# Gate probabilities of the top two logits: two sigmoids on ScalarE in place of a difference, an exponential with sum, and a reciprocal

## The chip, the cores and the metric

The kernel runs on one core of a Trainium2 chip. The metric is the device time of one execution in microseconds (us), as the median of several runs. The engines are TensorE (PE in the profile, with its weight loads as PEld), VectorE (DVE), ScalarE (ACT), GpSimd (POOL) and SyncE (SP), which here only issues DMAs.

## The reference

The input x is 8 tiles of 128 tokens by 512 features. A linear layer with a per-tile LoRA adapter comes first, then a feed-forward layer with a mixture of 8 LoRA experts, of which each token uses its two best. Cut to what matters:

```python
# cond: base layer plus the adapter of this tile
base_out = jnp.einsum('bsi,io->bso', x, W)
lora_out = jnp.einsum('bsr,bro->bso', jnp.einsum('bsi,bir->bsr', x, A), Bm)
c = base_out + lora_out
# ffn, E=8 experts, R=16, TOP_K=2, SCALING=1.0
result = jnp.einsum('bnd,od->bno', c, W_base) + b_base
logits = jnp.einsum('bnd,ed->bne', c, W_gate)
probs = jax.nn.softmax(logits, axis=-1)
top_p, top_i = jax.lax.top_k(probs, TOP_K)
top_p = top_p / jnp.sum(top_p, axis=-1, keepdims=True)
route_w = jnp.sum(jax.nn.one_hot(top_i, E) * top_p[..., None], axis=-2)
h = jnp.einsum('bnd,erd->bner', c, A_ffn)
delta = jnp.einsum('bner,eor->bno', h * route_w[..., None], B)
return x + result + delta * SCALING
```

Only the ratio of the two best probabilities survives the division by their sum. With the two largest logits v0 and v1, the two weights are 1/(1+exp(v1-v0)) and exp(v1-v0)/(1+exp(v1-v0)), which are sigmoid(v0-v1) and sigmoid(v1-v0).

## The kernel before, in words

All matmuls are made of three products of operands that are split in a high and a low part (x_hi and x_lo and so on): lines 811, 812 and 813 are the three products of the helper `product`. ScalarE writes the high parts, VectorE subtracts them from the raw values to get the low parts (the helper `lo`, line 597).

Up to about 28 us both layers are folded into one matrix. Then the 8 tiles (t = 0 to 7) are worked on in pairs (q = 0 to 3). The first two pairs (q = 0, 1 in the names `Left`, `Right`) are plain; pairs 2 and 3 use seven products in place of eight (`M1` to `M7`). For each pair TensorE forms the left bank of each tile (which holds the 8 logits, the 128 values h and part of the output), transposes the adapter activations (`T1`, line 923), and adds their contribution (`Lora_left`, line 937, which reports lg_done; `Lora_right`, line 944). From then on the logits of both tiles are complete and the gate can run. The gate gives hw, the 128 values h times the expert weights. TensorE transposes hw (`T2(t)`, line 954) into one single bank that all tiles share, ScalarE casts it to hw_hi (line 511), VectorE subtracts to get hw_lo (`split_hw`, line 597), and `Delta(t)` adds the experts' output.

The order of work on every engine is written out by hand, in five programs; engines wait for each other by semaphores. What matters here:

- `T2(t)` waits for hw_done(t+1), that is for the gate of its own tile, and for hw_lo_done(t), that is for the low split of the tile before it, since both use the one bank. It stands in TensorE's queue between other products; if it waits, everything behind it waits.
- VectorE's queue: gate(0), gate(1), split_x_inner(2), split_xa(2), split_hw(0), split_xa(3), split_hw(1), split_cs(SUM1), then gate(2), gate(3), sum_e(2) (line 686), split_cs(SUM7) (cs_lo, line 597), split_xa(4) (lines 721 and 723), split_hw(2), and so on; at the end split_xd(3), gate(6), gate(7), split_hw(6), sum_u1(3), split_hw(7).
- ScalarE's queue around gates 2 and 3: copy_left(0), copy_left(1), exp_top(2), copy_right(0), copy_right(1), copy_m5(2) (line 524), exp_top(3), copy_m4(2) (line 528, which waits for `M4(2)` on TensorE), split_hw(2) (line 511), split_cs(SUM7), split_cs(SUM6) (line 484). sum_e(2) waits for copy_m4(2); the VectorE split_cs(SUM7) waits for ScalarE's.
- TensorE's queue: ... Left(2), T2(0), Left(3), T2(1), Delta(0), T1(1), Delta(1), Lora_left(1), M5(2), M4(2), T2(2), M3(2), M2(2), T2(3), Right(2), ..., M7(3), M6(3, first chunk), Lora_right(3), T2(7), Delta(6), M6(3, second chunk), Lora_right(3), Delta(7).

The gate of one tile on VectorE (`gate`, lines 731 to 751) is nine instructions in the trace: the eight largest logits in order (line 736, MAX8), their first two minus the first (line 737, a TENSOR_SCALAR with a scalar from memory), the positions of the largest (line 739, which the trace shows as MATCH_VALUE_LOAD and FIND_INDEX8), the comparison of the expert numbers with the two positions (line 740), the reciprocal of the sum (line 743), the one-hot rows times the exponentials (line 744), the sum of both rows (line 746), and h times the weights times the reciprocal (line 749, a SCALAR_TENSOR_TENSOR with a scalar from memory). ScalarE's `exp_top` (line 504) takes the exponential of the two differences and adds them up; the trace shows an ACTIVATE and an ACTIVATION_READ_ACCUMULATOR. The helper `step` makes VectorE wait for its own instruction before it issues the next.

Of the kernel before, what the change touches and what calls it, by code (L numbers as in the profile page):

```python
# [5 lines left out]
F32 = mybir.dt.float32  # L6
F32R = mybir.dt.float32r
U32 = mybir.dt.uint32
ALU = mybir.AluOpType
ACT = mybir.ActivationFunctionType  # L10

P = 128
# [3 lines left out]
R = 16  # L16
NA = 16
E = 8
# [6 lines left out]
TOP = 2  # L25
# [17 lines left out]
def adaln_ffn_kernel(nc, x_t, itok, fold_in, lora, ffn_b, bias, out):  # L43
    ctx = ExitStack()
    with ctx:
        def sb(name, shape, dt=F32):
            return ctx.enter_context(nc.sbuf_tensor(name, shape, dt))

        def sem(name):
            return ctx.enter_context(nc.semaphore(name))  # L50
# [39 lines left out]
        top_val = sb("top_val", [P, 2, 8])  # L90
        top_idx = sb("top_idx", [P, 2, 8], U32)
        top_diff = sb("top_diff", [P, 2, TOP])
        top_exp = sb("top_exp", [P, 2, TOP])
        top_sum = sb("top_sum", [P, 2, 1])
        top_rcp = sb("top_rcp", [P, 2, 1])
        onehot = sb("onehot", [P, 2, TOP, E])
        weighted = sb("weighted", [P, 2, TOP, E])
        route = sb("route", [P, 2, E])
        hw = sb("hw", [P, 2, ER])
# [3 lines left out]
        table_warm = sb("table_warm", [P, 1])  # L103
# [5 lines left out]
        def part(flat, at, *shape):  # L109
# [62 lines left out]
            sem("left_done"), sem("xa_hi_done"), sem("xa_done"), sem("t1_done"), sem("xa_t_done"))  # L172
        lg_done, lz_done, gate_step, diff_done, exp_done, hw_done = (
            sem("lg_done"), sem("lz_done"), sem("gate_step"), sem("diff_done"), sem("exp_done"), sem("hw_done"))
        t2_done, hw_hi_done, hw_lo_done = sem("t2_done"), sem("hw_hi_done"), sem("hw_lo_done")
# [31 lines left out]
        def left(t):  # L207
            return left_bank[t % 4]
# [204 lines left out]
        def scalar_program(act):  # L413
            act.dma_start(w_raw[:, 0, FIRST:D + GH], fold_in[0, :, FIRST:D + GH]).then_inc(w_first_loaded, DMA)
            nc.scalar.activation(table_warm[:], nc.const_aps.tensor(0.0, [P, 1], F32), ACT.Exp)
            act.wait_ge(w_first_loaded, DMA)
# [84 lines left out]

            def exp_top(t):
                act.wait_ge(diff_done, t + 1)
                nc.scalar.activation(top_exp[:, t % 2], top_diff[:, t % 2], ACT.Exp,  # L504
                                     accum_out=top_sum[:, t % 2]).then_inc(exp_done, 1)

# [27 lines left out]
            copy_xa_t(0)  # L534
            split_x_inner(2)
            exp_top(0)
            exp_top(1)
            act.wait_ge(x4_lo_done, 1)
# [9 lines left out]
            copy_left(1)  # L548
            exp_top(2)
            copy_right(0)  # L550
            copy_right(1)
            copy_m5(2)
            exp_top(3)
            copy_m4(2)
# [10 lines left out]
            copy_xa_t(2)  # L565
            exp_top(4)
            copy_left(2)
            copy_right(2)
            copy_left(3)
            copy_right(3)  # L570
            exp_top(5)
            copy_m5(3)
# [6 lines left out]
            copy_xa_t(3)  # L579
            exp_top(6)  # L580
            copy_left(4)
            copy_right(4)
            exp_top(7)
            copy_right(5)
# [8 lines left out]
        def vector_program(dve):  # L593
# [113 lines left out]
            def step(instruction):  # L707
                instruction.then_inc(gate_step, 1)
                steps[0] += 1
                dve.wait_ge(gate_step, steps[0])  # L710
# [20 lines left out]
            def gate(t):  # L731
                n = t % 2
                logits = left(t)[:, gate_cols(t)]
                h = left(t)[:, h_cols(t)].rearrange("p (e r) -> p e r", e=E)
                dve.wait_ge(lg_done, t // 2 + 1)
                step(nc.vector.max(top_val[:, n], logits))
                nc.vector.tensor_scalar(top_diff[:, n], top_val[:, n, 0:TOP], top_val[:, n, 0:1], None,  # L737
                                        ALU.subtract).then_inc(diff_done, 1)
                step(nc.vector.max_index(top_idx[:, n], top_val[:, n], logits))
                step(nc.vector.tensor_tensor(onehot[:, n], expert_id[:].unsqueeze(1).broadcast_to([P, TOP, E]),  # L740
                                             top_idx[:, n, 0:TOP].unsqueeze(2).broadcast_to([P, TOP, E]), ALU.is_equal))
                dve.wait_ge(exp_done, t + 1)
                nc.vector.reciprocal(top_rcp[:, n], top_sum[:, n])
                step(nc.vector.tensor_tensor(weighted[:, n], onehot[:, n],
                                             top_exp[:, n].unsqueeze(2).broadcast_to([P, TOP, E]), ALU.mult))
                step(nc.vector.tensor_tensor(route[:, n], weighted[:, n, 0, :], weighted[:, n, 1, :], ALU.add))
                if t >= 2:
                    dve.wait_ge(t2_done, t - 1)
                nc.vector.scalar_tensor_tensor(out=hw[:, n].rearrange("p (e r) -> p e r", e=E), in0=h,  # L749
                                               scalar=top_rcp[:, n], in1=route[:, n].unsqueeze(2).broadcast_to([P, E, R]),  # L750
                                               op0=ALU.mult, op1=ALU.mult).then_inc(hw_done, 1)

# [374 lines left out]
```

## Time and profile before

| what | value |
|---|---|
| median of 3 runs | 66.19 us |
| the 3 runs | 66.19, 65.9, 66.25 us |
| the profiled execution | 65.62 us |
| its span, first to last instruction | 64.4 us |
| what lies around the span | 1.2 us |
| mean granted TensorE clock | 1.000 |
| TensorE busy | 59.6 us, 92% |
| VectorE busy | 49.2 us, 76% |
| ScalarE busy | 34.2 us, 53% |
| GpSimd busy | 23.7 us, 37% |

The times in the rows of the profile are from this one profiled execution and are counted from the start of its span. A matmul's row lasts from its start until its modelled end; the next one starts before that, since they are pipelined. So TensorE's progress is read from the starts of successive rows, or from the chain of waits, in which each piece is only what that matmul adds.

### The profile page before, as it was taken

To read this page: it belongs to the slowest core of one execution; us is meant where nothing else is said; L and a number is where in the kernel's file an instruction comes from. 1 tells how busy PE (TensorE), PEld (TensorE's weight loads), DVE (VectorE), ACT (ScalarE), POOL (GpSimd) and SP (SyncE) were. 2 spreads that over 40 slices of the span, in tenths; PEclk is the share of its full clock that TensorE was granted. 3 is DMA by queue.
4 is the path that set the end of the run, shared out by engine and by line. 5 is a ranking of instruction groups with operands and counts; after the bars stand their busy time and mean duration, and the time that the engine had idled before them with its cause. 6 is when DMAs were issued, how large, how long until landed. Compare 5 with 4: busy or idle time off the path is not lost.

```text
span 64.4 us, 1331 instructions
## 1 busy us (share of the span) xinstructions
PE 59.6 (92%) x406; PEld 58.0 (90%) x406; DVE 49.2 (76%) x154; ACT 34.2 (53%) x91; POOL 23.7 (37%) x46
## 2 busy tenths in 40 slices
PE   4979999999999999999999999979999999999900
PEld 4969999999999999999998999959999999998800
DVE  0948689955799989999889748969788668887510
ACT  1754689807399577074161756847094723355220
POOL 1000999798400799997039960000000000001300
DMA  0799999700998106233331323630008000023371
GB/s 0 210 362 300 371 377 404 276 0 20 320 294 320 42 12 188 60 73 63 66 81 37 72 62 74 222 132 0 0 0 300 29 6 0 0 89 116 121 279 52
DMA packets 5529, 8.75 MB, mean 136 GB/s; under 512 B 1009, under 2 KB 2065, under 8 KB 5522
## 3 DMA queue, kind: packets, MB, share of 16 engines
q1 hardware_dynamic: 4978, 7.88, 38.4%
q0 software_dynamic: 256, 0.52, 2.2%
q10 hardware_dynamic: 288, 0.27, 1.2%
q8 instruction: 3, 0.05, 0.3%
q14 instruction: 4, 0.03, 0.2%
HBM read 5.26 MB, written 2.10 MB: 114 GB/s over the span
## 4 chain that ended last, share of the span: by engine, by line
PE 81%; DVE 6%; DMA 5%; issue 2%; ACT 1%; DVEq 0%
PE bank L811 19%; PE bank L813 19%; PE bank L812 19%; PE bank L819 8%; PE bank L821 5%; DMA w_raw<-fold_in 5%; PE bank L985 3%; PE bank L937 2%; PE bank L954 2%; PE bank L944 1%; PE bank L989 1%; DVE cs_lo L597 1%; PE bank L923 1%; DVE top_diff L737 1%; DVE hw L749 1%
## 5 line engine op out<-in xcount | busy, mean ns | idle before, releaser
L811 PE MATMUL bank<-c_hi,x_hi 128*128 128x408 f32 (+1 forms) x40 | 13.6, 339 | 0.0
L812 PE MATMUL bank<-c_lo,x_hi 128*128 128x408 f32 (+1 forms) x40 | 13.4, 334 | 0.0
L813 PE MATMUL bank<-c_hi,x_lo 128*128 128x408 f32 (+1 forms) x40 | 13.4, 334 | 0.0
L398 POOL TENSOR_TENSOR x_raw<-x_raw 128x256 f32<-128x256 f32 x1 | 0.7, 739 | 21.3 <-DVE x_raw L703 21.3
L597 DVE TENSOR_TENSOR x_lo<-x_raw,x_hi 128x512 fp32r<-128x512 f32 (+1 forms) x10 | 7.8, 808 | 0.0
L811 PEld LDWEIGHTS bank<-c_hi,x_hi 128*128 128x128 f32 x40 | 7.5, 188 | 0.1
L812 PEld LDWEIGHTS bank<-c_lo,x_hi 128*128 128x128 f32 x40 | 7.5, 188 | 0.0
L813 PEld LDWEIGHTS bank<-c_hi,x_lo 128*128 128x128 f32 x40 | 7.5, 188 | 0.0
L331 POOL DMA_DIRECT2D lora_raw<-lora x8 | 4.4, 554 | 6.1 <-issue 5.9
L504 ACT ACTIVATE top_exp<-top_diff 128x2 f32<-128x2 f32 x8 | 1.6, 203 | 8.1 <-DVE top_diff L737 8.1
L811 PE MATMUL bank<-ffn_b_hi,hw_hi 128*128 128x256 f32 x16 | 4.8, 298 | 0.0
L813 PE MATMUL bank<-ffn_b_hi,hw_lo 128*128 128x256 f32 x16 | 4.5, 282 | 0.0
L812 PE MATMUL bank<-ffn_b_lo,hw_hi 128*128 128x256 f32 x16 | 4.5, 282 | 0.0
L597 DVE TENSOR_TENSOR wg_lo<-w_raw,wg_hi 128x648 fp32r<-128x648 f32 (+2 forms) x5 | 3.4, 695 | 0.7 <-ACT wg_hi L425 0.6
L511 ACT CAST hw_hi<-bank 128x128 fp32r<-128x128 f32 x8 | 2.1, 265 | 3.1 <-PE bank L954 3.1
L811 PE MATMUL bank<-cs_hi,x_hi 128*128 128x256 f32 x12 | 3.7, 310 | 0.0
L419 ACT CAST wt_hi<-w_raw 128x512 fp32r<-128x512 f32 x4 | 2.5, 620 | 2.2 <-DMA w_raw<-fold_in 2.0
L597 DVE TENSOR_TENSOR hw_lo<-bank,hw_hi 128x128 fp32r<-128x128 f32 x8 | 2.3, 287 | 1.7 <-ACT hw_hi L511 1.7
L363 POOL TENSOR_TENSOR x_raw<-x_raw 128x256 f32<-128x256 f32 x2 | 1.9, 956 | 4.5 <-DMA x_raw<-x_t 4.5
L979 PE MATMUL bank<-const-bfloat16-1.0 128*128 128x128 bf16 x24 | 2.7, 309 | 0.9 <-PEq L1120 0.9
L515 ACT COPY w_raw<-bank 128x256 f32<-128x256 f32 x8 | 2.9, 374 | 1.3 <-PE bank L813 1.2
L813 PE MATMUL bank<-cs_hi,x_lo 128*128 128x256 f32 x12 | 3.4, 281 | 0.0
(140 smaller groups left out, 192.0 us busy)
## 6 DMA issues: line engine op xcount, KB each, us to landing
x_raw<-x_t SPq DMA_DIRECT2D x8, 256.0 KB, 4.7
out<-w_raw SPq DMA_DIRECT2D x7, 256.0 KB, 2.0
w_raw<-fold_in SPq DMA_DIRECT2D x4, 256.0 KB, 5.0
w_raw<-fold_in SPq DMA_DIRECT2D x3, 324.0 KB, 5.0
bw_rows<-bw_hi SPq DMA_DIRECT2D x16, 40.5 KB, 2.1
lora_raw<-lora POOLq DMA_DIRECT2D x8, 64.0 KB, 4.1
bw_rows<-bw_lo SPq DMA_DIRECT2D x8, 40.5 KB, 2.1
ffn_b_raw<-ffn_b SPq DMA_DIRECT2D x1, 256.0 KB, 6.5
```

The lines of the kernel that those rows point to most:

```text
L331: pool.dma_start(lora_raw[:, b, :], lora[bass.ds(adapters[b], 1), :, :].rearrange("a p c -> (a p) c")).then_inc(lora_loaded, DMA)
L419: nc.scalar.copy(wt_hi[:, m, :], raw_wt(m)).then_inc(w_hi_done, 1)
L511: nc.scalar.copy(hw_hi[:, t % 2, :], t2_bank[:, 0:P]).then_inc(hw_hi_done, 1)
L515: nc.scalar.copy(y_out[:, t, y_of_left_bank(t)], left(t)[:, in_left_bank(t)]).then_inc(yl_done, 1)
L597: nc.vector.tensor_tensor(out, raw, hi.bitcast(F32), ALU.subtract).then_inc(done, 1)
L811: nc.tensor.matmul(out, a_hi, b_hi, start=first, stop=False, skip_group_check=True)
L812: nc.tensor.matmul(out, a_hi, b_lo, start=False, stop=False, skip_group_check=True)
L813: return nc.tensor.matmul(out, a_lo, b_hi, start=False, stop=last, skip_group_check=True)
L819: nc.tensor.matmul(bank[i][:, cols], w[:, m, rows], wg[:, m, cols], start=False, stop=False, skip_group_check=True)
L821: nc.tensor.matmul(fold_right(i), w[:, m, rows], wg[:, m, LEFT:], start=False, stop=False, skip_group_check=True)
L979: nc.tensor.matmul(bwr_bank[:, 0:P], ones, ones, start=True, stop=True)
L985: nc.tensor.matmul(bank[i][:, 0:GH], w_raw[:, 0, i * P:(i + 1) * P], raw_gh(0), start=True, stop=False, skip_group_check=True)
```

## The change

The gate keeps its order. The subtraction (line 737) and the reciprocal (line 743) are taken out of VectorE's program. MAX8 now reports top_done, on which both ScalarE and VectorE wait. ScalarE makes two activations of one column each: a sigmoid with scale -1 of the one logit, with the other logit as bias (a per-partition column from memory), in both orders. VectorE waits for both, multiplies them into the one-hot rows, and the last instruction becomes a plain product of two tensors. The activation at the start, which brings the function table into ScalarE, is changed from Exp to Sigmoid.

```diff
@@ -89,10 +89,7 @@
-        top_diff = sb("top_diff", [P, 2, TOP])
-        top_exp = sb("top_exp", [P, 2, TOP])
-        top_sum = sb("top_sum", [P, 2, 1])
-        top_rcp = sb("top_rcp", [P, 2, 1])
+        top_prob = sb("top_prob", [P, 2, TOP])
@@ -412,7 +409,7 @@
-            nc.scalar.activation(table_warm[:], nc.const_aps.tensor(0.0, [P, 1], F32), ACT.Exp)
+            nc.scalar.activation(table_warm[:], nc.const_aps.tensor(0.0, [P, 1], F32), ACT.Sigmoid)
@@ -499,10 +496,12 @@
-            def exp_top(t):
-                act.wait_ge(diff_done, t + 1)
-                nc.scalar.activation(top_exp[:, t % 2], top_diff[:, t % 2], ACT.Exp,
-                                     accum_out=top_sum[:, t % 2]).then_inc(exp_done, 1)
+            def prob_top(t):
+
+                act.wait_ge(top_done, t + 1)
+                for n in range(TOP):
+                    nc.scalar.activation(top_prob[:, t % 2, n:n + 1], top_val[:, t % 2, 1 - n:2 - n], ACT.Sigmoid,
+                                         bias=top_val[:, t % 2, n:n + 1], scale=-1.0).then_inc(prob_done, 1)
@@ -733,22 +732,19 @@
                 dve.wait_ge(lg_done, t // 2 + 1)
-                step(nc.vector.max(top_val[:, n], logits))
-                nc.vector.tensor_scalar(top_diff[:, n], top_val[:, n, 0:TOP], top_val[:, n, 0:1], None,
-                                        ALU.subtract).then_inc(diff_done, 1)
+                nc.vector.max(top_val[:, n], logits).then_inc(top_done, 1)
+                dve.wait_ge(top_done, t + 1)
                 step(nc.vector.max_index(top_idx[:, n], top_val[:, n], logits))
                 step(nc.vector.tensor_tensor(onehot[:, n], expert_id[:].unsqueeze(1).broadcast_to([P, TOP, E]),
                                              top_idx[:, n, 0:TOP].unsqueeze(2).broadcast_to([P, TOP, E]), ALU.is_equal))
-                dve.wait_ge(exp_done, t + 1)
-                nc.vector.reciprocal(top_rcp[:, n], top_sum[:, n])
+                dve.wait_ge(prob_done, 2 * t + 2)
                 step(nc.vector.tensor_tensor(weighted[:, n], onehot[:, n],
-                                             top_exp[:, n].unsqueeze(2).broadcast_to([P, TOP, E]), ALU.mult))
+                                             top_prob[:, n].unsqueeze(2).broadcast_to([P, TOP, E]), ALU.mult))
                 step(nc.vector.tensor_tensor(route[:, n], weighted[:, n, 0, :], weighted[:, n, 1, :], ALU.add))
                 if t >= 2:
                     dve.wait_ge(t2_done, t - 1)
-                nc.vector.scalar_tensor_tensor(out=hw[:, n].rearrange("p (e r) -> p e r", e=E), in0=h,
-                                               scalar=top_rcp[:, n], in1=route[:, n].unsqueeze(2).broadcast_to([P, E, R]),
-                                               op0=ALU.mult, op1=ALU.mult).then_inc(hw_done, 1)
+                nc.vector.tensor_tensor(hw[:, n].rearrange("p (e r) -> p e r", e=E), h,
+                                        route[:, n].unsqueeze(2).broadcast_to([P, E, R]), ALU.mult).then_inc(hw_done, 1)
```

The eight calls of `exp_top` become calls of `prob_top` at the same places of ScalarE's queue, and the semaphores diff_done and exp_done become top_done and prob_done.

## Rows read from the trace of the kernel before

**Rows 1.** The page's part on busy time, share of the span, instructions.

```profile
PE 59.6 (92%) x406; PEld 58.0 (90%) x406; DVE 49.2 (76%) x154; ACT 34.2 (53%) x91; POOL 23.7 (37%) x46
```

**Rows 2.** Timeline of weight loads (start, length, instruction, idle before): T2(1), T2(3), T2(7).

```profile
35.46 0.14 PEld L954 LDWEIGHTS bank<-ident,hw 128*128 128x128 f32 x1 [0.29 <-issue]
...
42.70 0.14 PEld L954 LDWEIGHTS bank<-ident,hw 128*128 128x128 f32 x1 [0.68 <-issue]
...
58.99 0.14 PEld L954 LDWEIGHTS bank<-ident,hw 128*128 128x128 f32 x1 [0.17 <-issue]
```

**Rows 3.** Chain of waits (start, added time, what): T2(1), T2(3), T2(6), T2(7).

```profile
35.52 0.28 PE bank L954
...
42.73 0.30 PE bank L954
...
57.72 0.11 PE bank L954
...
59.02 0.30 PE bank L954
```

**Rows 4.** Timeline of TensorE: last product of M4(2), last product of M2(2).

```profile
39.70 0.35 PE L813 MATMUL bank<-c_hi,x_lo 128*128 128x408 f32 x1
...
42.02 0.35 PE L813 MATMUL bank<-c_hi,x_lo 128*128 128x408 f32 x1
```

**Rows 5.** Timeline of VectorE: gate(2) whole, and the start of gate(3).

```profile
37.85 0.17 DVE L736 MAX8 top_val<-bank 128x8 f32<-128x8 f32 x1 [0.84 <-PE bank L937]
38.06 0.23 DVE L737 TENSOR_SCALAR top_diff<-top_val 128x2 f32<-128x2 f32 x1
38.20 0.08 DVE L739 MATCH_VALUE_LOAD top_idx<-top_val,bank 128x8 f32 x1
38.27 0.16 DVE L739 FIND_INDEX8 top_idx<-top_val,bank 128x8 uint32<-128x8 f32 x1
38.47 0.17 DVE L740 TENSOR_TENSOR onehot<-expert_id,top_idx 128x16 f32<-128x16 f32 x1
38.72 0.16 DVE L743 RECIPROCAL top_rcp<-top_sum 128x1 f32<-128x1 f32 x1
38.80 0.16 DVE L744 TENSOR_TENSOR weighted<-onehot,top_exp 128x16 f32<-128x16 f32 x1
38.99 0.17 DVE L746 TENSOR_TENSOR route<-weighted 128x8 f32<-128x8 f32 x1
39.19 0.35 DVE L749 SCALAR_TENSOR_TENSOR hw<-bank,top_rcp,route 128x128 f32<-128x128 f32 x1
39.46 0.16 DVE L736 MAX8 top_val<-bank 128x8 f32<-128x8 f32 x1
```

**Rows 6.** Timeline of ScalarE: exp_top(2), copy_m4(2), both cs_hi casts, split_hw(6).

```profile
38.32 0.20 ACT L504 ACTIVATE top_exp<-top_diff 128x2 f32<-128x2 f32 x1 [0.78 <-DVE top_diff L737]
38.43 0.19 ACT L504 ACTIVATION_READ_ACCUMULATOR top_exp<-top_diff 128x1 f32 x1
...
40.13 0.35 ACT L528 COPY x_raw<-bank 128x256 f32<-128x256 f32 x1
...
40.53 1.15 ACT L484 CAST cs_hi<-w_raw 128x512 fp32r<-128x512 f32 x2
...
58.02 0.27 ACT L511 CAST hw_hi<-bank 128x128 fp32r<-128x128 f32 x1
```

**Rows 7.** ScalarE by line and form (count, total busy and mean ns): the casts of cs_hi.

```profile
L484 ACT CAST cs_hi<-w_raw 128x512 fp32r<-128x512 f32 x3 | 1.8, 626 | 0.0
```

**Rows 8.** Timeline of VectorE after gate(3): sum_e(2), split_cs(SUM7), split_hw(2).

```profile
41.06 0.42 DVE L686 TENSOR_TENSOR x_raw<-x_raw 128x256 f32<-128x256 f32 x1
41.39 0.69 DVE L597 TENSOR_TENSOR cs_lo<-w_raw,cs_hi 128x512 fp32r<-128x512 f32 x1
...
42.30 0.28 DVE L597 TENSOR_TENSOR hw_lo<-bank,hw_hi 128x128 fp32r<-128x128 f32 x1
```

**Rows 9.** Timeline of ScalarE at the start: the only table load of the program.

```profile
1.30 1.28 ACT L415 ACT_TABLE_LOAD   x1 [1.30 <-PEq L1120]
```

More of the change, by code:

```diff
@@ L172, in adaln_ffn_kernel @@
             sem("left_done"), sem("xa_hi_done"), sem("xa_done"), sem("t1_done"), sem("xa_t_done"))
-        lg_done, lz_done, gate_step, diff_done, exp_done, hw_done = (
-            sem("lg_done"), sem("lz_done"), sem("gate_step"), sem("diff_done"), sem("exp_done"), sem("hw_done"))
+        lg_done, lz_done, gate_step, top_done, prob_done, hw_done = (
+            sem("lg_done"), sem("lz_done"), sem("gate_step"), sem("top_done"), sem("prob_done"), sem("hw_done"))
         t2_done, hw_hi_done, hw_lo_done = sem("t2_done"), sem("hw_hi_done"), sem("hw_lo_done")
@@ L535, in scalar_program @@
             split_x_inner(2)
-            exp_top(0)
-            exp_top(1)
+            prob_top(0)
+            prob_top(1)
             act.wait_ge(x4_lo_done, 1)
@@ L548, in scalar_program @@
             copy_left(1)
-            exp_top(2)
+            prob_top(2)
             copy_right(0)
@@ L552, in scalar_program @@
             copy_m5(2)
-            exp_top(3)
+            prob_top(3)
             copy_m4(2)
@@ L565, in scalar_program @@
             copy_xa_t(2)
-            exp_top(4)
+            prob_top(4)
             copy_left(2)
@@ L570, in scalar_program @@
             copy_right(3)
-            exp_top(5)
+            prob_top(5)
             copy_m5(3)
@@ L579, in scalar_program @@
             copy_xa_t(3)
-            exp_top(6)
+            prob_top(6)
             copy_left(4)
             copy_right(4)
-            exp_top(7)
+            prob_top(7)
             copy_right(5)
```

## The prediction

> **What bounds the kernel now.** I read the page's busy times first: TensorE is busy for 92% of the span and VectorE for 76% [rows 1]. So VectorE's saved time counts only where TensorE stands still for it. The next view is the timeline of the weight loads from 30 us on, because a matmul that waits shows as idle time before its weight load. There are only three such places, and all three are transposes of hw: T2(1), T2(3) and T2(7) [rows 2]. The chain of waits says what each costs. A transpose that waits for nothing, T2(6), adds 0.11 us; T2(1) adds 0.28 and T2(7) adds 0.30 [rows 3]. That makes 0.17 us lost at T2(1) and 0.19 at T2(7). T2(3) follows the last product of M2(2), whose end is 42.02 + 0.35 = 42.37 [rows 4]; it ends at 42.73 + 0.30 = 43.03 [rows 3], so it took 0.66 where 0.11 would do: 0.55 lost. All together 0.91 us. That is the most that a shorter gate can give, from 65.62 us of the profiled execution.
>
> What the transposes wait for is the low split of the tile before, on VectorE: hw_lo(2) ends at 42.30 + 0.28 = 42.58 [rows 8] and the weight load starts at 42.70 [rows 2], a hand-over of 0.12. Two gates stand ahead of that split in VectorE's queue in each of the three places. The gate is the thing to shorten; the question is what is late next.
>
> **The gate on VectorE.** One gate lasts from MAX8 at 37.85 to the next at 39.46, 1.61 us [rows 5]. The other pairs look the same. Its parts by their starts: MAX8 to difference 0.21, difference to MATCH_VALUE_LOAD 0.14, to FIND_INDEX8 0.07, to the comparison 0.20, to the reciprocal 0.25, to the product with the one-hot rows 0.08, to the sum 0.19, to hw 0.20, hw to the next MAX8 0.27.
>
> What the change removes and adds:
>
> 1. The difference goes. MATCH_VALUE_LOAD takes its slot at 0.21 after MAX8, since the wait for MAX8 stays. The comparison starts at 0.21 + 0.07 + 0.20 = 0.48 and VectorE by itself would be ready for the product at 0.68, with another 0.20 for the step.
> 2. The sigmoids. ScalarE now starts from MAX8's end and not from the difference's: MAX8 lasts 0.17 and the hand-over is 38.32 - (38.06 + 0.23) = 0.03 [rows 5, 6], so the first starts at 0.20. The trace has no activation with a bias from memory. From below, each is like the exponential here, 0.20 us, the second 0.11 behind the first [rows 6]: both done at 0.51. From above, I take each at 0.28 and no overlap: 0.76; the 0.28 is 0.20 plus 0.08, a little over the 0.06 to 0.07 that a scalar from memory costs VectorE (0.23 against 0.17 for a small operation, 0.35 against 0.28 for 128x128 [rows 5, 8]). I take 0.27 each with the overlap of 0.09 that the exponential and its read-out show: second starts 0.18 behind the first, both done at 0.65. VectorE goes on 0.10 after ScalarE's end, as it did for the reciprocal (38.62 to 38.72 [rows 5, 6]). So the product starts at 0.75 (bounds 0.68, where VectorE itself is last, and 0.86); it is at 0.95 now. A gain without any limit below 0.68 is excluded, because VectorE's own steps take that long.
> 3. The reciprocal goes: its 0.08 is in the above.
> 4. hw becomes a plain product. Now 0.35 long with the next start 0.27 behind; hw_lo, same size from the same kind of bank, is 0.28 long [rows 8]. That is 0.07 less: 0.20.
>
> The gate becomes 0.75 + 0.19 + 0.20 + 0.20 = 1.34 us (bounds 1.27 and 1.45), against 1.61. That is 0.27 less each (0.16 to 0.34), 2.2 us of VectorE in all.
>
> The trace shows no bias from memory on ScalarE, and a rule speaks against it: the Trainium skill, "ScalarE: Activation LUTs", section "What ACT_TABLE_LOAD costs", says that each per-partition operand from memory adds about 93 ns to an activation of 186 ns, and that successive ones overlap by about 93 ns. By that the pair would be done at 0.20 + 0.19 + 0.28 = 0.67, an estimate from that page, and the gate 1.36. It would change nothing below.
>
> **Place 1, T2(1).** Gates 0 and 1 give 0.54 us (at least 0.32) and hw_lo(0) needs only the 0.17 and a little more. split_xa(2) and hw_hi(0), which stand ahead, have long had their inputs. So the 0.17 goes, and all of TensorE behind it shifts by 0.17. What follows it (hw_hi(1), hw_lo(1), Delta(1)) hangs on T2(1) and shifts with it, and so does Lora_left(1), which releases gate 2 [rows 5].
>
> **Place 2, T2(3).** This is the largest part, and here another engine is next. VectorE would start sum_e(2) at 41.06 - 0.17 - 2 x 0.27 = 40.35 and could start the split of cs (line 597, SUM7) 0.33 later [rows 8], at 40.68. But it needs cs_hi from ScalarE. That starts at 40.53 and one cast takes 0.63 [rows 6, 7], so it is ready at 41.16 even now, only 0.23 before VectorE's use at 41.39. How far does ScalarE move? In front of cs_hi are split_hw(2) and copy_m4(2), at 40.13 [rows 6]. copy_m4(2) needs M4(2), whose last product ends at 39.70 + 0.35 = 40.05 [rows 4], 39.88 after the shift. With the hand-over of 0.03 to 0.04 it can start at 39.92: 0.21 earlier. The sigmoids of gate 3 are out of its way: MAX8 of gate 3 at 37.68 + 1.34 = 39.02, second sigmoid done at 39.67. So cs_hi is ready at 41.16 - 0.21 = 40.95 and the split starts at 40.98, 0.41 earlier than now and not 0.71. hw_lo(2) and T2(3) follow 0.41 earlier. split_xa(4) between them waits for M3(2), which is over by then. This result holds as long as VectorE reaches the split before 40.98, that is for any gate up to 1.49 us, which is above my upper bound. Of the 0.55 lost at T2(3), 0.41 - 0.17 = 0.24 comes back and 0.31 stays. Everything from T2(3) on is 0.41 earlier. Between T2(3) and T2(7) no weight load waits, so gates 4 and 5 give VectorE idle time and nothing else; the cover is TensorE's own work of over 12 us.
>
> **Place 3, T2(7).** hw_lo(6) stands behind gates 6 and 7. These end at least 0.32 us earlier relative to TensorE. Next is hw_hi(6) on ScalarE, from 58.02 for 0.27 [rows 6], which hangs on TensorE through a copy ahead of it: hw_lo(6) could start at 58.32, end at 58.60, and T2(7)'s weight load start at 58.72 against 58.99 now [rows 2]. That is 0.27 earlier, more than the 0.19 that was lost. So the 0.19 goes whole. The last stores hang on Delta(7) and move along.
>
> **The sum.** 0.17 + 0.24 + 0.19 = 0.60 us. The profiled execution took 65.62, so it would take 65.02. It lies 0.57 under the median of 66.19, within its kind of scatter (the three runs span 0.35), and I carry the difference over: 66.19 - 0.60 = 65.59 us.
>
> **The table.** Its load at the start is 1.28 us [rows 9], of whichever function, and the first weights come later than its end; cost 0.
>
> **Rivals.**
>
> A. Only part comes back. T2(1) stays late by something that its waits hide, or the sigmoids fall in ScalarE's way ahead of copy_m4(2) and copy_right(5). Without the 0.17, copy_m4(2) gains only 0.04 and the split 0.19 to 0.21; with T2(7)'s 0.19 that is 0.39 us, 65.80; without T2(7) 0.20 us, 65.99. For it: ScalarE is near in both places by 0.2 to 0.3 us. Against: the queues give no such wait.
>
> B. More comes back: ScalarE isn't last at T2(3), and all 0.91 us goes: 65.28. Against it stands the 0.63 of the cast in ScalarE's queue.
>
> C. Slower: the sigmoids are late. VectorE waits for both, and behind that wait stand the rest of the gate, the next gate and the low split for which TensorE waits. The point from which it turns is the product's present start, plus the 0.07 of hw: ready at 1.02, which is a pair that takes 0.72 us on ScalarE where I take 0.45. If a pair takes 1.0 us, a gate is 0.28 longer than now; T2(1) and T2(3) come 0.56 later each and T2(7) up to 0.56, 1.7 us in all: 67.9. For it: no row shows a bias from memory. Against: no operation of so few columns in the trace is over 0.2 on ScalarE.
>
> D. The sigmoid shares no table with the copies and casts around it, so that every gate brings a load of 1.28 us [rows 9]. Then the product starts at 2.03, each gate is about 1.0 longer, and three places times two gates give 6 us: about 72. In the trace the exponential lives with copies, casts and scaled activations on one load. The Trainium skill, "ScalarE: Activation LUTs", section "Table sets: the hidden batching unit", warns that functions of different sets cost a load at every switch, and also says that cheap functions such as copy are in every set; by that this doesn't happen.
>
> **Chances.** The forecast 0.60. A 0.20, of which a third is still over 0.5% faster. B 0.05. Nothing measurable, for a reason not listed, 0.05. C 0.08, D 0.02. A measurement of this kernel can tell about 0.5%, 0.33 us, from no change, so the lines are at 65.86 and 66.52. Faster: 0.60 + 0.07 + 0.05 less 0.02 for scatter = 0.70. Same: 0.13 + 0.05 + 0.02 = 0.20. Slower: 0.10. The range takes in B at the lower end and A with some scatter above: 65.2 to 66.25. The bounds of the sigmoids don't widen it, since the limits at T2(3) and T2(7) are elsewhere.
>
> **What would show it.** The gate's period in VectorE's timeline should be 1.34 (1.27 to 1.45), hw 0.28 long. Sigmoids of some 0.27 start 0.20 behind MAX8. Only T2(3) should still show a wait before its weight load, and ahead of it the cs split should wait for ScalarE's cast. T2(1) and T2(7) should add 0.11 in the chain. There should be one table load. The forecast is wrong if T2(1) still waits, if a new wait shows between T2(3) and T2(7), or if a gate takes over 1.49.

## The result and the profile after

The changed kernel took 64.41 us as the median of 4 runs (63.74 to 64.75), the kernel before 66.06 us beside it (4 runs, 65.9 to 66.25). The ratio is 0.967, with a 95% interval of 0.960 to 0.974; ratios here and below leave out runs over 1.5% above the fastest of their kernel, medians take in all, so the two need not divide evenly: this ratio rests on 63.74 and 64.07 alone, and the two medians give 0.975. I had forecast 65.59 us with a range of 65.2 to 66.25. The sign was right; the gain of 1.65 us is nearly three times the forecast 0.60. Two repetitions later gave 0.985 (0.976 to 0.993) and 0.978 (0.973 to 0.984), so part of that factor is scatter. The forecast 0.60 us would be 0.991: the last repetition lies clear of it, the interval of the other just reaches it.

| | before | after | after, third time |
|---|---|---|---|
| profiled execution | 65.62 us | 64.74 us | 64.36 us |
| span | 64.44 us | 63.55 us | 63.17 us |
| start, up to T1(0) | 28.65 | 29.09 | 28.71 |
| middle, T1(0) to the end of the last product | 32.57 | 32.12 | 32.12 |
| tail, from there to the end of the span | 3.22 | 2.34 | 2.34 |

The last three lines cut the span at two places of TensorE's timeline: the start of the first adapter transpose, T1(0), and the modelled end of the last product. The start lies ahead of everything that the change touches, but for the name of the function in the first activation, whose table load takes 1.28 us in both kernels. It is 28.07 to 29.53 in the profiles of this study, without order by kernel: the same changed kernel has 29.09, 29.45 and 28.71. TensorE's first twelve products behind the first weights account for it. They begin at 3.85 to 4.04 everywhere, the thirteenth product follows after 1.71 us in the kernel cs_early below and after 3.14 us in best14, and from there to T1(0) it is 22.41 to 22.54 in all fourteen profiles. The first eight of the twelve, in cs_early and in best14:

```profile
3.95 1.19 PE L981 MATMUL bank<-w_raw 128*128 128x136 f32 x8 [0.33 <-DMA w_raw<-fold_in]
```

```profile
3.94 2.18 PE L985 MATMUL bank<-w_raw 128*128 128x136 f32 x8 [0.32 <-DMA w_raw<-fold_in]
```

The profile shows a granted clock of 1.00 in this stretch of both, so why the pace differs stays open. But this stretch alone spreads the times of one and the same kernel over 1.46 us. The third profile has about the start of the one before, so that pair is the clean one: of its 1.27 us, 0.45 are in the middle, where I forecast 0.60, and 0.88 are in the tail, where I forecast nothing; the start takes 0.06 back.

For the middle, the starts of the same matmul rows in two kernels, counted from T1(0), say where TensorE gained on the kernel before. The numbers are the sum up to that place, in us:

| gained by the end of | T2(1) | T2(3) | T2(7) |
|---|---|---|---|
| forecast | 0.17 | 0.41 | 0.60 |
| after | 0.00 | 0.23 | 0.45 |
| pad16, below | 0.16 | 0.38 | 0.60 |

Busy times on the page of the kernel after, which answer to [rows 1]:

```profile
PE 59.9 (94%) x406; PEld 58.5 (92%) x406; DVE 47.4 (75%) x138; ACT 35.9 (57%) x91; POOL 23.5 (37%) x46
```

The weight loads of the hw transposes that still waited, which answer to [rows 2]. T2(7) is no longer among them:

```profile
35.89 0.14 PEld L950 LDWEIGHTS bank<-ident,hw 128*128 128x128 f32 x1 [0.27 <-issue]
...
42.91 0.14 PEld L950 LDWEIGHTS bank<-ident,hw 128*128 128x128 f32 x1 [0.45 <-issue]
```

The chain of waits of the kernel after (start, added time, what) for T2(1), T2(3) and T2(7), as in [rows 3]:

```profile
35.97 0.26 PE bank L950
...
42.94 0.30 PE bank L950
...
59.17 0.11 PE bank L950
```

T2(7) adds the 0.11 of a transpose that waits for nothing, as forecast. T2(3) still waits, as forecast. T2(1) adds 0.26 where I said 0.11.

VectorE's gate(2) in the kernel after, with the start of gate(3) (beside [rows 5]):

```profile
38.28 0.17 DVE L735 MAX8 top_val<-bank 128x8 f32<-128x8 f32 x1 [0.83 <-PE bank L933]
...
39.07 0.18 DVE L741 TENSOR_TENSOR weighted<-onehot,top_prob 128x16 f32<-128x16 f32 x1
39.28 0.17 DVE L743 TENSOR_TENSOR route<-weighted 128x8 f32<-128x8 f32 x1
39.48 0.29 DVE L746 TENSOR_TENSOR hw<-bank,route 128x128 f32<-128x128 f32 x1
39.69 0.17 DVE L735 MAX8 top_val<-bank 128x8 f32<-128x8 f32 x1
```

The period is 39.69 - 38.28 = 1.41 us, against 1.61 before. ScalarE's pair for gate(2), and copy_m4(2) with both cs_hi casts (beside [rows 6]):

```profile
38.49 0.48 ACT L503 ACTIVATE top_prob<-top_val 128x1 f32<-128x1 f32 x2 [0.51 <-DVE top_val L735]
...
40.50 0.37 ACT L527 COPY x_raw<-bank 128x256 f32<-128x256 f32 x1
...
40.93 1.15 ACT L481 CAST cs_hi<-w_raw 128x512 fp32r<-128x512 f32 x2
```

And the view of DMAs from 61 to 65 us, which I had not read for the prediction. The first lines of each fence are queues (packets, MB, share), the last two are the last stores, with the time from issue to landing. Before:

```profile
q10 hardware_dynamic: 144, 0.13, 10.2%
q14 instruction: 1, 0.01, 0.8%
...
out<-w_raw SPq DMA_DIRECT2D x1, 128.0 KB, 2.0
out<-w_raw ACTq DMA_DIRECT2D x1, 128.0 KB, 2.8
```

After:

```profile
q10 hardware_dynamic: 144, 0.13, 9.8%
...
out<-w_raw SPq DMA_DIRECT2D x1, 128.0 KB, 1.8
out<-w_raw ACTq DMA_DIRECT2D x1, 128.0 KB, 1.9
```

The same stores, but before a packet of a queue named "instruction" lies among them and is gone after. The trace gives its start as 62.75, its size as 8 KB and its length as 0.54 us. ScalarE's store has its first packet at 62.62 in both kernels and its last one ends at 63.90 before and 63.16 after. The store has 144 packets, nine for each of the 16 DMA engines. From 63.2 to 64 us the kernel before still has two packets of SyncE's store and nine of ScalarE's to move; the kernel after has none there:

```profile
q10 hardware_dynamic: 9, 0.01, 5.0%
q1 hardware_dynamic: 2, 0.00, 0.4%
```

They go one after another, SyncE's from 63.28, where the instruction packet ends (62.75 + 0.54 = 63.29), ScalarE's from 63.33 to 63.89. So one sixteenth of the store waits behind the instruction packet, and the store lands with it. The trace doesn't name the DMA engine of a packet; that all of these share one is read from the counts and the times.

### The profile page after: what moved, and what is told of

It is laid out like the page before. It is cut to its first block, busy times and chain, and to the rows that moved or that the text cites. A ratio compares the mean times of both kernels' runs of the same rounds, so it can differ in the third digit from the quotient of the medians.

```text
span 63.5 us, 1315 instructions
## 1 busy us (share of the span) xinstructions
PE 59.9 (94%) x406; PEld 58.5 (92%) x406; DVE 47.4 (75%) x138; ACT 35.9 (57%) x91; POOL 23.5 (37%) x46
## 4 chain that ended last, share of the span: by engine, by line
PE 86%; DMA 5%; issue 2%; ACT 2%; DVE 1%
PE bank L807 20%; PE bank L809 20%; PE bank L808 20%; PE bank L815 8%; PE bank L817 6%; DMA w_raw<-fold_in 5%; PE bank L981 3%; PE bank L933 2%; PE bank L950 2%; PE bank L940 2%; PE bank L985 1%; ACT cs_hi L481 1%; PE bank L919 1%; ACT w_raw L514 1%; PE bank L996 1%
## 5 line engine op out<-in xcount | busy, mean ns | idle before, releaser
L395 POOL TENSOR_TENSOR x_raw<-x_raw 128x256 f32<-128x256 f32 x1 | 0.7, 736 | 20.7 <-DVE x_raw L702 20.7
L596 DVE TENSOR_TENSOR x_lo<-x_raw,x_hi 128x512 fp32r<-128x512 f32 (+1 forms) x10 | 7.3, 752 | 0.0
L503 ACT ACTIVATE top_prob<-top_val 128x1 f32<-128x1 f32 x16 | 3.8, 288 | 5.8 <-DVE top_val L735 5.7
L596 DVE TENSOR_TENSOR wt_lo<-w_raw,wt_hi 128x512 fp32r<-128x512 f32 x4 | 2.8, 688 | 1.3 <-ACT wt_hi L416 1.3
```

What stands on the lines that cost most here:

```text
L503: nc.scalar.activation(top_prob[:, t % 2, n:n + 1], top_val[:, t % 2, 1 - n:2 - n], ACT.Sigmoid, bias=top_val[:, t % 2, n:n + 1], scale=-1 ...
L596: nc.vector.tensor_tensor(out, raw, hi.bitcast(F32), ALU.subtract).then_inc(done, 1)
```

## Where the runs stand

Every kernel of the study, middle and tail from its one profiled execution. "Records" are VectorE's instructions listed in the trace, its waits included. "Packet" is the start of the last 8 KB instruction packet, where one comes after 50 us.

| kernel | records | packet | middle | tail | median us, runs | ratio to before, 95% |
|---|---|---|---|---|---|---|
| before | 190 | 62.75 | 32.57 | 3.22 | 66.06, 4 | |
| after | 174 | none | 32.12 | 2.34 | 64.41, 4 | 0.967 (0.960 to 0.974) |
| after_again | 174 | none | 32.26 | 2.34 | 64.72, 4 | 0.985 (0.976 to 0.993) |
| after_third | 174 | none | 32.12 | 2.34 | 64.26, 6 | 0.978 (0.973 to 0.984) |
| pad16 | 190 | 62.70 | 31.97 | 3.08 | 65.34, 10 | 0.988 (0.982 to 0.994) |
| pad8 | 182 | none | 32.54 | 2.35 | 64.44, 4 | 0.979 (0.969 to 0.990) |
| norcp | 182 | none | 32.35 | 2.35 | 64.61, 10 | 0.980 (0.975 to 0.985) |
| before_pad24 | 214 | 57.07 | 32.73 | 2.35 | 65.06, 12 | 0.994 (0.989 to 0.999) |
| before_pad7 | 197 | 60.74 | 33.00 | 2.35 | 65.91, 1 | |
| after_pad40 | 214 | 56.67 | 32.13 | 2.33 | 64.22, 6 | 0.980 (0.972 to 0.988) |
| cs_early | 174 | none | 32.23 | 2.34 | 63.83, 4 | 0.974 (0.966 to 0.982) |
| cs_both | 174 | none | 31.82 | 2.34 | 64.34, 6 | 0.982 (0.978 to 0.986) |
| best14 | 188 | 64.79, behind the span's end | 31.68 | 2.33 | 64.29, 6 | 0.981 (0.976 to 0.985) |
| before_cs | 190 | 62.09 | 32.01 | 3.33 | 65.09, 10 | 0.988 (0.983 to 0.993) |

Ratios are against the runs of the kernel before on the same chip, and its medians there were 65.4 to 66.1.

## The experiments

### The change once more

No edit, on another chip.

> The changed kernel once more. Theory F (my main one now): VectorE's program is 16 instructions shorter, and an 8 KB instruction packet that before stood at 62.75 us in the middle of the last stores is gone; the last store then lands 1.9 us after its issue and not 2.8. So the page shows 3 packets of queue 14 and not 4, and what lies between the last product of TensorE (end about 61.2) and the end of the span is about 2.3 us and not 3.2. Theory M (my prediction's): all comes from the waits of T2(1), T2(3) and T2(7), 0.60 us; the tail then is as before, about 3.2 us, and its shortness in the first profile was chance. The time is 0.967 of before in either case. A side question: the wait of 0.54 us in gate 1 for the sigmoids (33.25 to 33.79, though the second sigmoid had ended at 33.28) is there again if it has a fixed cause, and is gone if it was chance.

Ratio 0.985, span 64.1. Its start stretch is 29.45, 0.80 longer than in the kernel before, and middle and tail are as in the first profile within 0.15. So the gain of 1.65 us in the first comparison has a lucky part. The starts are wide enough to hold it: middle, tail and the 1.2 us around the span, with the shortest and the longest start of the study, make 65.0 to 66.5 us for the kernel before and 63.7 to 65.2 for the kernel after, and the first comparison set 65.9 to 66.25 against 63.74 to 64.75. The short tail is no part of the luck.

### The VectorE program made as long as before

A satisfied wait does no work. Two of them make one record in the trace, and such records follow each other 0.098 us apart. Here are 16 such records, in places where VectorE has time:

```diff
             nc.vector.memset(bw_rows[:, 0].bitcast(F32), 0.0).then_inc(even_zeros, 1)
+            for _ in range(16):
+                dve.wait_ge(even_zeros, 1)
...
+            for _ in range(16):
+                dve.wait_ge(even_zeros, 1)
             dve.wait_ge(ident_ready, 1)
```

> The changed kernel with 16 instructions added to VectorE that do nothing (waits on a semaphore long raised), 8 after its first memset and 8 ahead of the fold's diagonal, both places where it idles. VectorE's program is as long as before's again. Theory F: the fourth packet of queue 14 is back at about 62.7, the last store takes 2.8 us, and 0.9 us of the gain is lost: 0.985 to 0.99 of before. Theory M: the padding lies in idle time, the packets don't matter, the time is that of the changed kernel, 0.967.

The work is that of the changed kernel, and the long tail of the kernel before is back, with its packet. The DMAs of pad16 from 61 to 65 us:

```profile
q14 instruction: 1, 0.01, 0.8%
...
out<-w_raw SPq DMA_DIRECT2D x1, 128.0 KB, 2.0
out<-w_raw ACTq DMA_DIRECT2D x1, 128.0 KB, 2.6
```

The middle is 31.97, which is 0.60 less than before's 32.57, and the table of gains above has the three forecast terms at their places within 0.03: the whole forecast, in the kernel where the changed gate meets a program of the old length. Chain of waits of pad16, T2(1), T2(3), T2(7):

```profile
36.08 0.11 PE bank L954
...
42.91 0.30 PE bank L954
...
59.14 0.11 PE bank L954
```

Here T2(1) adds its 0.11 too. Its ten times lie in two groups, 64.35 to 64.87 and 65.28 to 65.61, and the profiled one is in the upper. They don't tell of the packet: norcp below has the same gap in its ten times, 64.67 to 65.22, with a short tail in its profile, and before_cs has a long tail in a profile of its lower group (64.83). The starts of the study with pad16's own middle and tail make 64.3 to 65.8 us, which takes in all ten. For the same reason the timed ratios alone would not show the tail's part: pad16's 0.988 and after_again's 0.985, taken together on one chip, have intervals that overlap. It rests on the profiles. So two things lie between my sum and the measured time: the tail, and something at T2(1) in the kernel after that goes with the same 16 records.

### Half as many

As pad16, with `range(8)` in both places.

> The changed kernel with 8 such instructions, half in each place. It is the control for the padding's own cost. Theory F: the time is either that of the changed kernel (0.967) with 3 packets of queue 14, or that of the one with 16 (about 0.987) with 4 packets, with nothing between; the packet and the time go together. Theory M: 0.967 and the packets as they like. If the padding itself cost time, this would lie half way.

With 182 records there is no packet in the tail and the tail is short, 2.35. But the middle is 32.54. Of the 0.42 more than after, 0.39 is lost at Lora_left(0), ahead of the first gate, in a profile with an early start (28.18). The rest of TensorE's rows go as in the kernel after, T2(1)'s wait included, and VectorE's gate(0) shows a gap that wasn't there. Comparison and product of that gate in pad8:

```profile
31.16 0.17 DVE L742 TENSOR_TENSOR onehot<-expert_id,top_idx 128x16 f32<-128x16 f32 x1
31.87 0.17 DVE L745 TENSOR_TENSOR weighted<-onehot,top_prob 128x16 f32<-128x16 f32 x1 [0.54 <-ACT top_prob L503]
```

The same two rows of the kernel after, in gate(1), and ScalarE's pair:

```profile
33.08 0.17 DVE L738 TENSOR_TENSOR onehot<-expert_id,top_idx 128x16 f32<-128x16 f32 x1
33.79 0.32 DVE L741 TENSOR_TENSOR weighted<-onehot,top_prob 128x16 f32<-128x16 f32 x1 [0.54 <-ACT top_prob L503]
```

```profile
32.80 0.48 ACT L503 ACTIVATE top_prob<-top_val 128x1 f32<-128x1 f32 x2 [0.92 <-DVE top_val L735]
```

The profile puts the gap down to ScalarE, but the second sigmoid ends at 32.80 + 0.48 = 33.28, and the product starts 0.51 after that where gate(2) needs 0.10. In both kernels that product is VectorE's 64th record. In pad16 the 64th record is not one that follows a wait for another engine, and gate(1) runs through:

```profile
33.19 0.18 DVE L742 TENSOR_TENSOR onehot<-expert_id,top_idx 128x16 f32<-128x16 f32 x1
33.50 0.17 DVE L745 TENSOR_TENSOR weighted<-onehot,top_prob 128x16 f32<-128x16 f32 x1
```

### The old gate without the reciprocals

The eight reciprocals are left out of the kernel before, so that the weights are multiplied by the sum in place of being divided by it. That leaves 182 records without any sigmoid.

```diff
-                nc.vector.reciprocal(top_rcp[:, n], top_sum[:, n])
...
-                                               scalar=top_rcp[:, n], in1=route[:, n].unsqueeze(2).broadcast_to([P, E, R]),
+                                               scalar=top_sum[:, n], in1=route[:, n].unsqueeze(2).broadcast_to([P, E, R]),
```

> The kernel before with the reciprocals left out and nothing else changed (the weights are multiplied by the sum and not divided by it, so that part of the computation is left out). VectorE's program is 8 instructions shorter, a gate about 0.08 us. Theory M: the waits at T2(1), T2(3), T2(7) shrink by 0.16 each at most, 0.3 to 0.45 us in all: 0.993 to 0.995 of before. Theory F: if 8 fewer are enough for the packet to go, the last store lands 0.9 us sooner and the ratio is about 0.98; if not, the packet stays and the ratio is as by theory M.

The tail is 2.35: it goes by the records, not by the sigmoids. The middle is 32.35, 0.22 less than before for some 0.08 less per gate.

### Is it length, or place?

The kernel before with 24 more idle records: 6 after the memset, 8 after the bias's low part, 4 ahead of `ident_ready` and 6 ahead of gate(2). A theory that a long program has a long tail (L) expects the tail to stay or grow. A theory by place expects the last packet to be asked for sooner and to be out of the way.

> The kernel before, with 24 instructions added to VectorE that do nothing, in places where it idles (after its first memset, ahead of the low parts of lora, ahead of the diagonal, ahead of gate 2). Theory F (an 8 KB instruction packet among the last stores): the packet is asked for when VectorE reaches a fixed place of its program; 24 more instructions bring that place forward, out of the tail to about 57 us. Page: 4 packets of queue 14 still, none after 61 us; from TensorE's last end to the end of the span 2.35 us and not 3.18; 0.8 us faster than before, ratio 0.988, with more instructions and nothing else changed. Theory L (a shorter VectorE program is faster for another reason, such as less work): no gain, ratio 1.000 or above.

Packet at 57.07, tail 2.35. From 57 to 58 us, and then ScalarE's store from 61 to 65 us:

```profile
q14 instruction: 1, 0.01, 2.5%
```

```profile
out<-w_raw ACTq DMA_DIRECT2D x1, 128.0 KB, 1.9
```

Theory L falls by the profile: more instructions, and a tail 0.87 shorter than before. The time agrees, though only just: 0.994 (0.989 to 0.999). With the middle 0.16 longer, 0.7 us were to be expected and the ratio gives 0.4; the starts scatter by more than that difference. Whether all executions of the kernel before have the long tail is not shown; only one of them has a profile.

### A pause put into the kernel before

Seven idle records in the kernel before (3 after the memset, 4 after the bias's low part) make gate(0)'s reciprocal, which follows the wait for ScalarE, the 64th.

> The kernel before with 7 such instructions. In it the 64th instruction is then the reciprocal of gate 0, which comes right behind a wait for ScalarE, like the instruction that pauses in the changed kernel. If the pause belongs to the place in the program and to a wait ahead of it, the reciprocal of gate 0 starts 0.47 us behind its wait and not 0.065. If it belongs to the sigmoids, there is none. Theory F also says: the last packet is asked for 7 instructions sooner, at about 60 us; if it is served before 62 us the tail is 2.35 us.

From the profile of its one execution: the reciprocal starts 0.473 after the wait ahead of it, where that takes 0.065 otherwise. Gate(0) of before_pad7:

```profile
32.09 0.17 DVE L744 TENSOR_TENSOR onehot<-expert_id,top_idx 128x16 f32<-128x16 f32 x1
32.75 0.16 DVE L747 RECIPROCAL top_rcp<-top_sum 128x1 f32<-128x1 f32 x1 [0.49 <-DVE onehot L744]
```

So the pause is one of the place and not of the sigmoid or the product. The middle is the longest of all, 33.00; TensorE falls 0.44 behind the kernel before, all of it at T2(1). A second gap of 0.74 us stands at the 192nd and 193rd records, where TensorE waits for nothing. The packet came at 60.74 and the tail is 2.35.

### Forty records in the kernel after

8, 10, 10 and 8 records at the four places of before_pad24, and 4 more ahead of split_hw(4): 214 in all.

> The changed kernel with 40 such instructions, in the same places and ahead of a late low split. Its VectorE program is as long as that of the padded kernel before. Theory F: no packet after 61 us, tail 2.35 us as in the changed kernel. The pause of 0.41 us that VectorE takes ahead of the 64th instruction of its program (gate 1 in the changed kernel, gate 0 with 8 added) then falls among long instructions, T2(1) doesn't wait, and the stretch from T1(0) to TensorE's last end is 31.97 us as with 16 added, against 32.11 to 32.26 in the changed kernel. Ratio to before 0.978 or lower: 0.60 by the gates and 0.8 by the tail. If padding costs time after all, the ratio is above that of the changed kernel.

The 64th record is in a harmless place, but the 192nd is now gate(6)'s product, and the pause is there:

```profile
56.02 0.17 DVE L747 TENSOR_TENSOR weighted<-onehot,top_prob 128x16 f32<-128x16 f32 x1 [0.50 <-ACT top_prob L503]
```

64 and 192 are 128 apart. Against the kernel after, TensorE is 0.16 ahead from T2(1) on and loses it again at T2(7), whose weight load at 58.44 waits 0.16, so that the middle is the same within 0.01.

### The 0.31 us left at T2(3)

ScalarE's casts for SUM7 and SUM6 moved up in the kernel after, out of the queue behind copy_m4(2), which I had named as the next limit:

```diff
             split_cs(SUM1, 2)
+            split_cs(SUM7, 4)
+            split_cs(SUM6, 1)
...
             split_hw(2)
-            split_cs(SUM7, 4)
-            split_cs(SUM6, 1)
```

> The changed kernel with ScalarE's two casts of cs_hi (SUM7 and SUM6) moved ahead, from behind split_hw(2) to behind the cast of SUM1, where ScalarE idles 1.7 us. Theory of my prediction (at T2(3) the cast on ScalarE is last, and VectorE's split of cs waits for it): the split starts at once after sum_e(2), 0.16 us sooner, and the 0.32 us that T2(3) still loses becomes 0.16. Rival (VectorE's own work alone decides): T2(3) loses 0.32 as now.

Chain of cs_early, T2(3) then T2(7):

```profile
42.08 0.26 PE bank L950
...
58.27 0.11 PE bank L950
```

From the end of M2(2)'s last product, T2(3) now loses 0.15 where it lost 0.32 in the kernel after. ScalarE was the limit there; the next is VectorE's own queue. The middle as a whole, 32.23, is no shorter, because 0.23 was lost at Lora_left(0), ahead of the gates, again with an early start (28.07), and 0.05 at T2(1). So in cs_both VectorE's split_cs(SUM7, 2) moves up as well, from behind sum_e(2) to behind split_cs(SUM1, 1).

> The changed kernel with ScalarE's two casts of cs_hi moved ahead as in cs_early, and VectorE's split_cs(SUM7) moved from behind sum_e(2) to ahead of gate 2, where VectorE idles 0.8 us. By my theory of T2(3) (first ScalarE's cast, then VectorE's own queue), T2(3) then waits for nothing and adds 0.11 us, against 0.26 with the casts alone. The middle, from T1(0) to TensorE's last end, is 0.15 us shorter than cs_early's 32.23. Rival (M3(2) or the bank is last at T2(3)): no change against cs_early.

```profile
36.29 0.26 PE bank L950
...
43.12 0.11 PE bank L950
...
59.19 0.11 PE bank L950
```

T2(3) waits for nothing and the middle is 31.82. T2(1) still has the pause. With 14 idle records (6 after the memset, 8 ahead of the low parts of `lb`) the pause should go and the last packet should not come back into the stores:

> cs_both with 14 instructions that do nothing, ahead of the gates, so that the 64th instruction of VectorE's program is the long low split of x ahead of gate 0. Theory P (the pause belongs to the 64th place, and long instructions around it hide it): gate 1 and gate 0 show no wait of 0.5 us, T2(1) adds 0.11 us, and the middle is another 0.15 to 0.2 us shorter, about 31.9. VectorE's program has 188 recorded instructions then, between 182 (no packet in the tail) and 190 (packet in the tail): if the packet is there the tail is 3.1 us and the ratio 0.98, if not it is 2.3 us and the ratio about 0.965, below every kernel so far.

```profile
36.40 0.11 PE bank L954
...
43.10 0.11 PE bank L954
...
59.18 0.11 PE bank L954
```

Nothing waits any more. Middle and tail together are 34.01 us, against 34.46 after and 35.79 before. Yet its measured time, 64.29, can't be told from cs_early's 63.83, cs_both's 64.34 or the change's own 64.26: the start of its profile is 29.53, the longest of the study, and this stretch varies by more than what is left to gain. Its last packet starts at 64.79, 1.25 us behind the end of the span, and not among the stores.

### The moves without the change

Both moves of cs_both in the kernel before, with the old gate.

> The kernel before with the three moves of cs_both. T2(3) loses 0.55 us in the kernel before; by my theory the queue of VectorE alone then ends hw_lo(2) at 41.98 for a weight load at 42.10 where 42.02 would be free, so that at most 0.1 us is still lost: 0.45 us faster, ratio 0.993, from the moves alone. The tail keeps its packet and its 3.2 us. If the two gates were what held T2(3), and not the cast behind them, less than half of that comes back.

```profile
35.15 0.28 PE bank L954
...
42.03 0.11 PE bank L954
...
58.12 0.30 PE bank L954
```

T2(3)'s whole wait of 0.55 goes by order alone, and T2(1) and T2(7) keep theirs, which need a shorter gate. The middle is 0.55 shorter, the tail still 3.33, with a packet at 62.09. The ratio is 0.988, like that of pad16, which has the new gate and the long tail: two different gains, 0.55 and 0.60 us by their profiles, and neither includes the tail.

### The change a third time

> The changed kernel once more, since the two ratios so far (0.967 and 0.985) have intervals that don't overlap, and the stretch up to T1(0), whose code the change doesn't touch but for one function name, ran from 28.1 to 29.5 us over the profiles. Theory of the parts: middle 32.57 to 32.2 (0.3 to 0.5 us less) and tail 3.18 to 2.35 (0.85 less), 1.15 to 1.35 us in all, ratio 0.980 to 0.983, with the start as chance has it. Rival (the change also shortens the start): ratio near 0.967 again, and T1(0) clearly under the 28.65 us of the kernel before.

0.978 (0.973 to 0.984), about 1.4 us. Middle 32.12 and tail 2.34 repeat the first profile.

## Why the prediction was right and wrong

**The step that failed** is the last sentence of place 3: "The last stores hang on Delta(7) and move along." I took the end of the program as a fixed length behind TensorE. It was 3.22 us before and 2.34 in all five profiles with 174 records: 0.88 us of gain that the sum put at nothing. The three profiles with an instruction packet among the last stores (before, pad16, before_cs) have tails of 3.08 to 3.33; the eleven without have 2.33 to 2.35, with 174 to 214 records, with either gate. The packet's place moved as the count of records moved. That the removed instructions shift it is shown, and so is what it holds up: in all three, nine packets of ScalarE's store, a sixteenth of it, start one at a time right behind the instruction packet, when the rest of the store is over, and the store lands 2.6 to 2.9 us after its issue in place of 1.9. That the change took the packet out of the tail was luck: its sixteen instructions fewer were meant to shorten the gate, and idle instructions undid it in pad16 and did the same in before_pad24. A view of SyncE's waits (total, times, longest) would have made me ask. Its wait for its store before was

```profile
SPq L325 <- DMA out<-w_raw: 2.7, 1, 2.7
```

and that of the kernel after is

```profile
SPq L322 <- DMA out<-w_raw: 1.8, 1, 1.8
```

**The sum.** The middle was forecast at 0.60 less, and it came out at 0.45 in the kernel after and at 0.60 in pad16. The missing part is T2(1)'s, by the table of gains. I wrote that "the queues give no such wait", and they don't: the product paused 0.41 us because it was the 64th record right behind a wait. Rival A allowed for "something that its waits hide" and was right for that one place. It priced the split without T2(1)'s 0.17 at 0.19 to 0.21, where my own working gives 0.41 - 0.17 = 0.24, and 0.23 is what T2(3) gained. The pause is seen at that place in all three profiles of the change, in cs_early and cs_both, in pad8 at gate(0), in before_pad7 at another instruction, and not in pad16 or best14.

**T2(3).** Forecast: 0.31 stays lost. Measured: M2(2)'s last product,

```profile
42.46 0.35 PE L809 MATMUL bank<-c_hi,x_lo 128*128 128x408 f32 x1
```

ends at 42.81 and T2(3) at 42.94 + 0.30 = 43.24; less 0.11 that is 0.32. The reason, ScalarE's cast behind copy_m4(2), held in cs_early. Rival B, that all of it comes back, fell.

**T2(7).** Forecast: the 0.19 goes whole. It adds 0.11.

**The gate.** Forecast 1.34, bounds 1.27 to 1.45, measured 1.41. The product starts 0.79 behind MAX8 (I said 0.75), the sigmoids start 0.21 behind it (0.20) and the pair takes 0.48 (0.45). hw is 0.29 long (0.28). The single sigmoids, by the trace of gate(1), are 0.297 and 0.282 long, 0.20 apart, where I took 0.27 and 0.18. The small misses add to 0.07 and changed nothing, as the limits were elsewhere. The Trainium skill, "ScalarE: Activation LUTs", section "What ACT_TABLE_LOAD costs", gives some 93 ns for an operand from memory; these rows against the exponential's 0.20 agree with it, and the 0.28 that I had worked out from it was nearer than my 0.27.

**Rivals C and D** fell: the pair takes 0.48 and not 0.72, and there is one table load:

```profile
1.31 1.28 ACT L412 ACT_TABLE_LOAD   x1 [1.31 <-PEq L1116]
```

**The chances** were in order, the range was not. It was built from TensorE's waits alone, and "all 0.91 us goes" was its lower end; the tail could not be in it.

## What to carry to other kernels

Ahead of a sum over waits, cut the span into start, middle and tail and look at what the DMA view shows in the tail: a gain of the same size as the change's own can sit there, and it can hang on the number of instructions and not on what they do. Test such a gain by adding idle instructions until the count is that of the kernel before; if it goes, it is a matter of placement and can be had, or lost, by any edit. Compare the starts as well, before a ratio of few runs is believed. When an engine becomes faster, reading which other engine's queue is late next (here a cast behind a copy) gave the remaining wait to 0.01 us, and moving that work up gave it back, also without the change.

## What the runs showed of the hardware

- Instructions are brought in by 8 KB DMA packets during the run. One among the last stores goes with a tail longer by 0.7 to 1.0 us; the store on ScalarE's queue then lands 2.6 to 2.9 us after its issue (before, pad16, before_cs), and 1.9 otherwise.
- Where VectorE has more than 190 records (before_pad24, before_pad7, after_pad40), the last 8 KB packet starts 0.64 to 0.65 us after the start of the 192nd. With 190 it starts 1.35 to 1.59 us after the end of VectorE's last instruction, with 188 (best14) 3.41 us after it, and with 182 or fewer none shows. What sets these times is not shown.
- VectorE pauses some 0.41 us at its 64th, and in after_pad40 at its 192nd, record when that stands right behind a wait for another engine. In the kernel after an instruction packet starts at 34.81, about 1.0 us after the paused product, and in the eight profiles with a pause it is 0.65 to 1.11 us. That both belong to the supply of instructions is argued from this and from the distance of 128, and not shown.
- Idle wait records of VectorE follow each other 0.098 us apart, and one record holds two waits.
- TensorE's first eight products behind the first weights take 1.19 us in one execution (cs_early) and 2.18 in another (best14, and the kernel after), at a granted clock of 1.00 in both. The cause is open.
- A product that normally takes 0.17 us took 0.32 in gate(1) of the kernel after, while GpSimd ran. In all five profiles where this product took 0.32 to 0.33 us, a tensor operation of GpSimd had begun 0.02 to 0.03 us before it. I didn't test this.
